# Attention kernel: the last two probability tiles of each half are added on VectorE, and TensorE's denominators take two sets of matmuls per half instead of three

## The chip, the core and the metric

The kernel runs on one core of a Trainium2 chip. A core has TensorE (PE in the profile, PEld for its weight loads), VectorE (DVE), ScalarE (ACT), GpSimd (POOL) and SyncE (SP), which here issues every transfer. All have their own instruction streams and meet at semaphores. The metric is the device time of one execution in microseconds (us).

## What is computed

The input x is 8 batches of 1024 tokens by 512 features. It is normalised by token; the result adds x, an attention block and a feed-forward block of ternary weights:

```python
xn = _layernorm(x, axis=-1)
x = x + _L0_attn_ref(xn, L0_attn_W_qkv, L0_attn_W_o) + _L0_ffn_ref(xn, L0_ffn_w_fc, L0_ffn_w_proj)
```

The attention has 16 heads of 32 features in each batch:

```python
scores = jnp.einsum('bhqd,bhkd->bhqk', Q, K) * D_H ** (-0.5)
attn = jax.nn.softmax(scores, axis=-1)
out = jnp.einsum('bhqk,bhkd->bhqd', attn, V)
```

The softmax divides each row of exponentials by its sum, the denominator. The change is in how these sums over the keys are formed.

## The kernel before, in words

Four stages follow one another: the weights (`weight_stage`), the tokens with the feed-forward block (`token_stage`), the attention (`attention_stage`), and the output projection (`output_stage`). Only the attention stage is touched.

**Groups, halves, units.** The 128 pairs of batch and head are taken four at a time: 32 groups (`GROUPS`), HG = 4 heads each. A group has two halves of 512 queries, and a half has 8 units, each with 128 keys (the keys lie on the partitions, the 512 queries along the free side). So a group has 16 units, w = 0 to 15; the first half is w = 0 to 7, the second w = 8 to 15. The probabilities of a unit are one tile `pr[:, w % 8]` of 128 x (4 heads x 512) float32, and there are 8 such slots.

**TensorE in one unit** (`body` under `@block.tensor`, L1019 to L1039). In this order: scores of head 0, one maxima matmul, scores of head 1, one maxima matmul, scores of head 2, then the denominators when the table `DEN` has an entry for this w, then the outputs of the unit before (`outputs`, L972), then a maxima matmul, scores of head 3, a maxima matmul. The maxima matmuls (`max_scores`, L985) are a second computation of scores, for a group ahead (the next one, and from w = 13 on the one after it), since the row maxima must be known before that group's exponentials. They are written to `psX`, which has three banks.

**VectorE** reduces each of these banks to row maxima (`maximum`, L919), 64 in a group, four in a unit. A maxima matmul waits on `max_done` until the reduction three before it is done (at the end of a group, two before: `bank_free`, L715). Between the reductions VectorE has a few small operations: `negate` at w = 13, `split_rows` at w = 14, `invert` at w = 7 and 15.

**ScalarE** takes the exponential of each scores bank (`exp`, L877) and copies outputs and denominators out of PSUM.

**GpSimd** adds the probability tiles 0 to 5 (`POOLED` = 6) of a half into `acc[:, hf]`, with five additions of 128 x 2048 (`add`, L849): the first at w % 8 = 1, once tiles 0 and 1 are there. It also multiplies the outputs by the inverse denominators (`normalise`, L858), at w = 2 and w = 9.

**The denominators** of a half are formed by TensorE in the following units (`denominators`, L1000): ones matrices times a probability tile, four matmuls of 32 output rows (one for each head) a set. `DEN_STEPS` is KT_N - POOLED + 1 = 3: one set for tile 6, one for tile 7, one for `acc`, all accumulated in `psM`. The table `DEN` puts them, for the second half of the group before, at w = 2, 3, 4, and for the first half of the same group at w = 10, 11, 12. ScalarE copies them out at w = 5 and 13.

The order of each engine is written out by hand in these `body` functions and tables. Two groups at the start and two at the end are unrolled, the 28 between them run in a loop of four groups a turn (`groups`, L739). In the last group there are no maxima any more, and behind it come the last denominators.

Of the kernel before, what the change touches and what calls it, by code (L numbers as in the profile page):

```python
# [28 lines left out]
ALU = mybir.AluOpType  # L29
# [25 lines left out]
HG = 4  # L55
GROUPS = B * H // HG
KT_N = L // P
UNITS = 2 * KT_N
# [3 lines left out]
POOLED = 6  # L62
# [10 lines left out]
def shift(g, d):  # L73
    return g + d if isinstance(g, int) else (g[0], g[1], g[2] + d)
# [576 lines left out]

DEN_STEPS = KT_N - POOLED + 1
X_LATE = 13
# [7 lines left out]
STORE = {3: (1, 0), 10: (1, 1)}  # L661
DEN = {2: (1, 1, 0), 3: (1, 1, 1), 4: (1, 1, 2), 10: (0, 0, 0), 11: (0, 0, 1), 12: (0, 0, 2)}
DEN_OUT = {5: (1, 1), 13: (0, 0)}
# [5 lines left out]
def attention_stage(nc, stack_dram, v_dram, ot_dram, den_dram, keep):  # L669
# [5 lines left out]
    with ExitStack() as ctx:  # L675
# [27 lines left out]
        s_full, exp_done, pv_done = sem("scores_full"), sem("exp_done"), sem("pv_done")  # L703
        added = sem("probs_added")
        den_stored, few_loaded, inverted = sem("den_stored"), sem("few_loaded"), sem("inverted")
# [212 lines left out]
        def _(dve):  # L918
# [13 lines left out]
            def split_rows(n):  # L932
# [5 lines left out]
                                               ALU.mult, ALU.subtract).then_inc(rows_ready, 1)  # L938

            def invert(g, hf):  # L940
                dve.wait_ge(few_loaded, lin(g, 32, 16 * hf + 16))
                wait(dve, inv_stored, lin(g, 32, 16 * hf - 16))
                nc.vector.reciprocal(rfew[:, hf, :], few[:, hf, :]).then_inc(inverted, 1)

            def body(g, units):
                for w in units:
                    for k, x in enumerate(maxima(g, w)):
                        if x:
                            maximum(*x)
                        if k == 0 and w == X_LATE and exists(shift(g, 1)):  # L950
                            negate(shift(g, 1))
                        if k == 0 and due(INVERT, g, w):
                            invert(*due(INVERT, g, w))
                        if k == 1 and w == ROWS_AT and exists(shift(g, 1)):
                            split_rows(shift(g, 1))

            nc.vector.memset(ones[:], AUG_UNIT).then_inc(ones_set, 1)
            groups(dve, body)
            invert(GROUPS - 1, 1)

        @block.tensor
        def _(pe):
# [37 lines left out]
            def denominators(g, hf, k):  # L1000

                if k == 0:
                    pe.wait_ge(exp_done, lin(g, PER_GROUP, HG * KT_N * (hf + 1)))
                    if hf == 0:
# [186 lines left out]
```

## Time and profile before

| | us |
|---|---|
| median of 3 runs | 3598.9 (3597.92 to 3601.58) |
| the profiled execution, whole | 3605.65 |
| its span, first to last instruction | 3603.8 |
| PE busy in the span | 3366.3 (93%) |
| DVE busy | 2345.0 (65%) |
| ACT busy | 1989.4 (55%) |
| POOL busy | 2076.2 (58%) |
| mean granted TensorE clock, share of full speed | 0.969 |

The attention stage takes from about 1619 us to 3362 us of the span. A busy engine is one that has an instruction in work; for PE, whose matmuls overlap, busy doesn't mean that it is at its peak. Instructions that follow one another closely on one engine overlap in the records by some hundredths of a microsecond; the distance from start to start is then what one takes of the engine's time.

### The profile page before, as it was taken

The numbers are of one execution on the slowest core, as the hardware profiler recorded it, in microseconds if no ns is written. First come the engines' busy times: TensorE is split into PE (matmuls) and PEld (weight loads), VectorE is DVE, ScalarE is ACT, GpSimd is POOL, SyncE is SP. The second block draws the span as 40 slices with busy tenths as digits, with TensorE's granted clock in tenths as the row PEclk, the third lists the DMA queues.
The fourth block names the chain that finished last, engine by engine and source line by source line (L and its number), as shares of the span: only waits on it lengthen the run. The fifth ranks groups of instructions, "written<-read, shape, count | busy, mean of one in ns | idle before, by whom it ended". The sixth has DMA issues, their size and how long they took to land. (4 is left out here: it accounts for less than half of the span.)

```text
span 3603.8 us, 57034 instructions
## 1 busy us (share of the span) xinstructions
PE 3366.3 (93%) x17648; PEld 1448.0 (40%) x17648; DVE 2345.0 (65%) x3431; ACT 1989.4 (55%) x2946; POOL 2076.2 (58%) x705
## 2 busy tenths in 40 slices
PE   3899999999999999989999999999999999999687
PEld 2444444444444444432333333333333333333466
DVE  6666666655666666668777777777777777773111
ACT  3444434433443443433877777777777777778111
POOL 0333332333332223314999898989989898999332
PEclk7999999999999999997999999999999999999799
DMA  4122222222222222133333333333233333321465
GB/s 163 71 76 86 71 86 72 85 85 78 79 81 89 81 80 72 82 79 68 81 70 68 78 73 69 72 78 71 68 78 75 65 75 74 76 64 31 147 226 198
DMA packets 376034, 308.49 MB, mean 86 GB/s; under 512 B 300672, under 2 KB 317056, under 8 KB 365440
## 3 DMA queue, kind: packets, MB, share of 16 engines
q1 hardware_dynamic: 375744, 304.69, 31.1%
q8 instruction: 174, 2.85, 0.3%
q14 instruction: 116, 0.95, 0.1%
HBM read 96.99 MB, written 139.46 MB: 66 GB/s over the span
## 5 line engine op out<-in xcount | busy, mean ns | idle before, releaser
L924 DVE TENSOR_REDUCE half_maxima<-scores_for_maxima 128x1 f32<-128x512 f32 x2048 | 1277.1, 682 | 370.1 <-PE scores_for_maxima L990 369.8
L887 ACT ACTIVATE probs<-scores,scalars 128x512 f32<-128x512 f32 x2048 | 1256.7, 689 | 423.8 <-PE scores L969 423.4
L855 POOL TENSOR_TENSOR probs_sum<-probs_sum,probs 128x2048 f32<-128x2048 f32 x256 | 1163.2, 4544 | 16.9
L990 PE MATMUL scores_for_maxima<-k_stackT,q_stackT 96*128 96x512 f16 x2048 | 804.1, 394 | 21.6 <-DMA q_stackT<-stack_scratch 11.2
L969 PE MATMUL scores<-q_stackT,k_stackT 98*128 98x512 f16 x2048 | 783.7, 385 | 27.6 <-issue 18.5
L981 PE MATMUL outputs<-probs,v_rows 128*32 128x512 f32 x4096 | 545.5, 605 | 1.2 <-ACT probs L887 0.8
L558 ACT ACTIVATE gelu_out<-psA,scalars 128x1024 f32<-128x1024 f32 x128 | 142.5, 1113 | 666.2 <-PE psA L607 666.2
L990 PEld LDWEIGHTS scores_for_maxima<-k_stackT,q_stackT 96*128 96x128 f16 x2048 | 200.5, 98 | 624.9 <-DVE half_maxima L924 468.1
L855 POOL TENSOR_TENSOR probs_sum<-probs 128x2048 f32<-128x2048 f32 x64 | 291.2, 4549 | 220.3 <-ACT probs L887 220.3
L969 PEld LDWEIGHTS scores<-q_stackT,k_stackT 98*128 98x128 f16 x2048 | 294.7, 145 | 241.5 <-ACT probs L887 46.5
L607 PE MATMUL psA<-x_hi,ternary_fcT 128*128 128x512 f16 x1024 | 388.2, 379 | 1.8 <-DVE x_lo L431 1.4
L607 PE MATMUL psA<-x_lo,ternary_fcT 128*128 128x512 f16 x1024 | 388.3, 379 | 0.0
L637 PE MATMUL psC<-ternary_projT,h_lo 128*128 128x512 f16 x1024 | 388.2, 379 | 0.0
L637 PE MATMUL psC<-ternary_projT,h_hi 128*128 128x512 f16 x1024 | 388.1, 379 | 0.0
L385 POOL TENSOR_TENSOR gelu_sum<-gelu_sum,gelu_out 128x1024 f32<-128x1024 f32 x96 | 256.4, 2671 | 194.9 <-ACT gelu_out L558 190.5
L385 POOL TENSOR_TENSOR gelu_sum<-gelu_out 128x1024 f32<-128x1024 f32 x16 | 41.0, 2563 | 554.2 <-ACT gelu_out L558 554.2
L593 PE MATMUL psB<-wqkvT_hi,x_hi 128*128 128x512 f16 x768 | 296.8, 386 | 50.7 <-DVE hi_hi_lo_hi_rows L424 50.6
L538 ACT ACTIVATE hi_hi_lo_hi_rows<-psB,qkv_scale 128x1024 f16<-128x1024 f32 x192 | 213.9, 1114 | 194.3 <-PE psB L593 194.3
L593 PE MATMUL psB<-wqkvT_lo,x_hi 128*128 128x512 f16 x768 | 296.8, 386 | 0.0
L593 PE MATMUL psB<-wqkvT_hi,x_lo 128*128 128x512 f16 x768 | 296.2, 386 | 0.0
L500 DVE SCALAR_TENSOR_TENSOR square_sum<-ternary_proj_sums,hidden_stats,psC 128x512 f32<-128x512 f32 x64 | 47.8, 747 | 319.2 <-PE psC L637 319.2
L454 DVE TENSOR_SCALAR h_hi<-gelu_out,scalars 128x1024 f16<-128x1024 f32 x128 | 167.7, 1310 | 134.1 <-ACT gelu_out L558 133.6
(123 smaller groups left out, 3313.2 us busy)
## 6 DMA issues: line engine op xcount, KB each, us to landing
stack_scratch<-hi_hi_lo_hi_rows SPq DMA_DIRECT2D x32, 1536.0 KB, 5.1
stack_scratch<-hi_hi_lo_hi_rows SPq DMA_DIRECT2D x32, 576.0 KB, 5.9
v_scratch<-v_rows_out SPq DMA_DIRECT2D x32, 576.0 KB, 6.9
x_rows<-in_L_attn_x SPq DMA_DIRECT2D x16, 1024.0 KB, 4.8
x_plus_ffn_scratch<-x_rows SPq DMA_DIRECT2D x16, 1024.0 KB, 3.9
v_rows<-v_scratch SPq DMA_DIRECT2D x32, 512.0 KB, 4.1
inverse_denominators<-denominators_scratch SPq DMA_DIRECT2D x256, 64.0 KB, 2.1
attention_scratch<-out_normed SPq DMA_DIRECT2D x64, 256.0 KB, 2.0
```

Source lines behind the costliest of these rows:

```text
L385: nc.gpsimd.tensor_tensor(gacc[:], g[:, 0, :] if j == 1 else gacc[:], g[:, j % 4, :], ALU.add).then_inc(g_added, 1)
L454: nc.vector.tensor_scalar(hh[:, pair, :], gj, S["inv1"], None, ALU.mult).then_inc(hh_ready, 1)
L538: nc.scalar.activation(stack[:, i % 2, heads, 0:2, :], rows.unsqueeze(2).to_broadcast([P, BANK // DH, 2, DH]), ACT.Copy, scale=rc[:, s, i: ...
L593: last = nc.tensor.matmul(psB[:, u % 2, :], xx[:, s, c, i * P:(i + 1) * P], keep[ww][:, c, cols], start=(k == 0), stop=(k == len(terms) - 1))
L607: last = nc.tensor.matmul(psA[:, 2 * (j % 2) + b, :], w, xx[:, s, c, :], start=(c == 0 and k == 0), stop=(c == CD - 1 and k == 1))
L637: last = nc.tensor.matmul(psC[:, (s + 5 + i) % 2, :], h[:, f, i * P:(i + 1) * P], keep["t2T"][:, f, :], start=(f == 0 and k == 0), stop=(f ...
L855: nc.gpsimd.tensor_tensor(acc[:, hf], pr[:, 0] if j == 1 else acc[:, hf], pr[:, j], ALU.add).then_inc(added, 1)
L887: nc.scalar.activation(pr[:, w % 8, h, :], psS[:, bank(HG * w + h), :], ACT.Exp, scale=keep["scal"]["escale"]).then_inc(exp_done, 1)
L924: nc.vector.tensor_reduce(mx[:, slot(n, 2), h, t, kh:kh + 1], psX[:, bank(r), :], axis=AX.X, op=ALU.max).then_inc(max_done, 1)
L969: nc.tensor.matmul(psS[:, bank(HG * w + h), :], kT[0:AUG, slot(g, 4), h, i:L:KT_N], qT[0:AUG, slot(g, 4), h, hf * BANK:(hf + 1) * BANK], s ...
L981: last = nc.tensor.matmul(psO[32 * h:32 * h + 32, :], v[:, slot(g, 2), h, i, :], pr[:, w % 8, h, :], start=(i == 0), stop=(i == KT_N - 1))
L990: nc.tensor.matmul(psX[:, bank(r), :], qT[0:STACK, slot(n, 4), h, t * P:(t + 1) * P], kT[0:STACK, slot(n, 4), h, kh * BANK:(kh + 1) * BANK ...
```

## The change

VectorE gets a new operation, `add_pair`: it adds tile 7 of a half onto tile 6, in place, 128 x 2048 float32 with both inputs in SBUF. A new table `PAIR` puts it after the second reduction of unit 9 (for the first half of the same group) and of unit 1 (for the second half of the group before), and once behind the last group. It waits until all exponentials of that half are done and until TensorE has used tile 6 for the outputs. TensorE's denominators have two sets, one for the summed tile and one for `acc`; the sets at w = 2 and w = 10 are gone, and the first of the two that are left waits for the new addition instead of for the exponentials.

```diff
-DEN_STEPS = KT_N - POOLED + 1
+DEN_STEPS = 2
...
-DEN = {2: (1, 1, 0), 3: (1, 1, 1), 4: (1, 1, 2), 10: (0, 0, 0), 11: (0, 0, 1), 12: (0, 0, 2)}
+PAIR = {1: (1, 1), 9: (0, 0)}
+DEN = {3: (1, 1, 0), 4: (1, 1, 1), 11: (0, 0, 0), 12: (0, 0, 1)}
...
-        added = sem("probs_added")
+        added, pair_added = sem("probs_added"), sem("last_pair_added")
...
+            def add_pair(g, hf):
+                dve.wait_ge(exp_done, lin(g, PER_GROUP, HG * KT_N * (hf + 1)))
+                dve.wait_ge(pv_done, lin(g, UNITS, 8 * hf + POOLED + 1))
+                nc.vector.tensor_tensor(pr[:, POOLED], pr[:, POOLED], pr[:, POOLED + 1], ALU.add).then_inc(pair_added, 1)
...
+                        if k == 1 and due(PAIR, g, w):
+                            add_pair(*due(PAIR, g, w))
...
             groups(dve, body)
+            add_pair(GROUPS - 1, 1)
             invert(GROUPS - 1, 1)
...
                 if k == 0:
-                    pe.wait_ge(exp_done, lin(g, PER_GROUP, HG * KT_N * (hf + 1)))
+                    pe.wait_ge(pair_added, lin(g, 2, hf + 1))
```

VectorE's order before, from unit 15 of the first group to unit 13 of the second (a row is an instruction, or so many equal ones):

```order
L924 TENSOR_REDUCE half_maxima<-scores_for_maxima 128x1 x3
L943 RECIPROCAL inverses_once<-denominators_once 128x16
L924 TENSOR_REDUCE half_maxima<-scores_for_maxima 128x1 x32
L943 RECIPROCAL inverses_once<-denominators_once 128x16
L924 TENSOR_REDUCE half_maxima<-scores_for_maxima 128x1 x24
L929 TENSOR_REDUCE negated_maxima<-half_maxima 128x32
```

and now the same stretch, where the lines of the kernel are one to six higher:

```order
L925 TENSOR_REDUCE half_maxima<-scores_for_maxima 128x1 x3
L949 RECIPROCAL inverses_once<-denominators_once 128x16
L925 TENSOR_REDUCE half_maxima<-scores_for_maxima 128x1 x9
L944 TENSOR_TENSOR probs<-probs 128x2048
L925 TENSOR_REDUCE half_maxima<-scores_for_maxima 128x1 x23
L949 RECIPROCAL inverses_once<-denominators_once 128x16
L925 TENSOR_REDUCE half_maxima<-scores_for_maxima 128x1 x9
L944 TENSOR_TENSOR probs<-probs 128x2048
L925 TENSOR_REDUCE half_maxima<-scores_for_maxima 128x1 x15
L930 TENSOR_REDUCE negated_maxima<-half_maxima 128x32
```

The new addition stands between reductions, once in each half, with 64 reductions for every two additions.

TensorE's order before, in unit 10 of a group, from its second maxima matmul (L1014 is a set of denominators, L981 the outputs of the unit before):

```order
L990 MATMUL scores_for_maxima<-k_stackT,q_stackT 128x512
L969 MATMUL scores<-q_stackT,k_stackT 128x512
L1014 MATMUL misc<-probs,ones 32x512 x4
L981 MATMUL outputs<-probs,v_rows 32x512 x4
L990 MATMUL scores_for_maxima<-k_stackT,q_stackT 128x512
```

and now, at the same place:

```order
L999 MATMUL scores_for_maxima<-k_stackT,q_stackT 128x512
L978 MATMUL scores<-q_stackT,k_stackT 128x512
L990 MATMUL outputs<-probs,v_rows 32x512 x4
L999 MATMUL scores_for_maxima<-k_stackT,q_stackT 128x512
L978 MATMUL scores<-q_stackT,k_stackT 128x512
```

One set of four matmuls has gone from unit 10, as from unit 2; nothing else of TensorE's order moved.

## Rows read from the trace of the kernel before

**Rows 1.** Page, costliest groups: busy us, mean ns | idle before, releaser.
```profile
L924 DVE TENSOR_REDUCE half_maxima<-scores_for_maxima 128x1 f32<-128x512 f32 x2048 | 1277.1, 682 | 370.1 <-PE scores_for_maxima L990 369.8
L855 POOL TENSOR_TENSOR probs_sum<-probs_sum,probs 128x2048 f32<-128x2048 f32 x256 | 1163.2, 4544 | 16.9
```
**Rows 2.** Windows: busy us of PE, PEld, DVE, ACT, POOL; clock, DMA. Group, last group.
```profile
2511.82:2563.47 51.65, 51.24 (x307) 18.28 (x306) 40.53 (x70) 40.67 (x69) 47.82 (x12) 1.00 0.36 74
3295.50:3347.70 52.20, 42.50 (x252) 12.05 (x250) 0.51 (x2) 39.01 (x66) 50.88 (x14) 0.99 0.08 22
```
**Rows 3.** Lines, shapes kept apart: denominator matmuls of tiles 6 and 7.
```profile
L1014 PE MATMUL misc<-probs,ones 128*32 128x512 f32 x1024 | 136.1, 604 | 0.0
```
**Rows 4.** Timeline (start us, us, instruction [idle before <-releaser]), PE and DVE, units 0 to 2.
```profile
2507.55 0.39 PE L990 MATMUL scores_for_maxima<-k_stackT,q_stackT 96*128 96x512 f16 x1
2507.98 2.48 DVE L924 TENSOR_REDUCE half_maxima<-scores_for_maxima 128x1 f32<-128x512 f32 x4 [0.70 <-PE scores_for_maxima L990]
2510.41 0.39 PE L990 MATMUL scores_for_maxima<-k_stackT,q_stackT 96*128 96x512 f16 x1
2510.84 2.49 DVE L924 TENSOR_REDUCE half_maxima<-scores_for_maxima 128x1 f32<-128x512 f32 x4 [0.38 <-PE scores_for_maxima L990]
2511.74 0.38 PE L990 MATMUL scores_for_maxima<-k_stackT,q_stackT 96*128 96x512 f16 x1
2512.26 1.07 PE L1014 MATMUL misc<-probs,ones 128*32 128x512 f32 x8
2514.12 0.39 PE L990 MATMUL scores_for_maxima<-k_stackT,q_stackT 96*128 96x512 f16 x1
```
**Rows 5.** Timeline of PE and DVE, units 12 and 13.
```profile
2495.67 1.89 DVE L924 TENSOR_REDUCE half_maxima<-scores_for_maxima 128x1 f32<-128x512 f32 x3 [1.22 <-PE scores_for_maxima L990]
2497.02 0.39 PE L990 MATMUL scores_for_maxima<-k_stackT,q_stackT 96*128 96x512 f16 x1 [0.29 <-DVE half_maxima L924]
2497.56 1.06 PE L981 MATMUL outputs<-probs,v_rows 128*32 128x512 f32 x8
```
**Rows 6.** Timeline of POOL, three halves.
```profile
2491.29 18.42 POOL L855 TENSOR_TENSOR probs_sum<-probs_sum,probs 128x2048 f32<-128x2048 f32 x4
2511.82 4.55 POOL L855 TENSOR_TENSOR probs_sum<-probs 128x2048 f32<-128x2048 f32 x1 [2.12 <-ACT probs L887]
...
2522.20 13.80 POOL L855 TENSOR_TENSOR probs_sum<-probs_sum,probs 128x2048 f32<-128x2048 f32 x3
2537.20 4.55 POOL L855 TENSOR_TENSOR probs_sum<-probs 128x2048 f32<-128x2048 f32 x1 [1.21 <-ACT probs L887]
```
**Rows 7.** Timeline of POOL and DVE in the token stage; a DVE addition without POOL.
```profile
795.18 5.11 POOL L385 TENSOR_TENSOR gelu_sum<-gelu_sum,gelu_out 128x1024 f32<-128x1024 f32 x2 [0.23 <-POOL qkv_scale L375]
798.01 3.37 DVE L440 TENSOR_TENSOR square_sum<-square_sum,gelu_squared 128x1024 f32<-128x1024 f32 x1
801.30 1.27 DVE L458 SCALAR_TENSOR_TENSOR h_lo<-gelu_out,scalars,h_hi 128x1024 f16<-128x1024 f32 x1
801.45 3.33 POOL L385 TENSOR_TENSOR gelu_sum<-gelu_sum,gelu_out 128x1024 f32<-128x1024 f32 x1 [1.16 <-ACT gelu_out L558]
...
3364.44 2.29 DVE L1136 TENSOR_TENSOR woT_lo<-woT,woT_hi 128x2048 fp32r<-128x2048 f32 x1 [10.49 <-ACT woT_hi L1099]
```
**Rows 8.** Timeline of PE where the loop starts its next turn.
```profile
2611.92 0.44 PE L969 MATMUL scores<-q_stackT,k_stackT 98*128 98x512 f16 x1 [3.42 <-issue]
...
2613.79 1.94 PE L981 MATMUL outputs<-probs,v_rows 128*32 128x512 f32 x8
```
**Rows 9.** Windows, columns as in rows 2: just behind that gap.
```profile
2613.00:2615.00 2.00, 2.00 (x11) 0.20 (x8) 1.00 (x2) 1.50 (x3) 0.00 (x0) 0.50 0.80 131
```
**Rows 10.** Timeline of POOL and PE in the last group.
```profile
3299.05 4.56 POOL L855 TENSOR_TENSOR probs_sum<-probs 128x2048 f32<-128x2048 f32 x1 [0.46 <-ACT probs L887]
3323.37 4.56 POOL L855 TENSOR_TENSOR probs_sum<-probs 128x2048 f32<-128x2048 f32 x1
3347.75 1.93 PE L1014 MATMUL misc<-probs_sum,ones 128*32 128x512 f32 x8 [4.05 <-POOL probs_sum L855]
```

## The prediction

> **What bounds the kernel now.** I began with the page's groups, for the load of the engine that gets the new work, then took the windows of one group, and then the timeline of the units in which something changes. In the steady part a group takes 51.65 us; TensorE is busy for 51.24 us of it, VectorE for 40.53, ScalarE for 40.67, GpSimd for 47.82, and the granted clock is 1.00 [rows 2]. TensorE is the bound, GpSimd is close behind. VectorE looks free: it waits 369.8 us in all for maxima banks [rows 1]. The question is in what pieces that idle time lies. The timeline shows it: four reductions in 2.48 us, then 0.38 us of idle in a unit of 2.86 us, which is the distance of the maxima matmuls at 2507.55 and 2510.41 [rows 4]. TensorE, in turn, has three banks for VectorE to be late in.
>
> What happens when they don't suffice is to be seen once in each group already. Near its end two maxima matmuls share a bank at a distance of two. There TensorE idles 0.29 us until a reduction is done, and starts at 2497.02, 0.06 us after the second of three reductions ended (the three end at 2497.56, and they lie 0.60 apart) [rows 5]. The outputs come 0.54 us behind that matmul; in the undisturbed unit the next set comes 0.52 us behind it [rows 4, 5]. So TensorE makes up for none of the delay: scores and outputs stand behind the waiting matmul in its order, and whoever delays that matmul delays the group.
>
> **What goes.** A set of denominators in unit 2 stretches the distance of the maxima matmuls from 2.86 to 3.71 us (2510.41 to 2514.12), so it takes 0.85 us of TensorE [rows 4]. The 1024 records of tile sets are 64 halves by 16 [rows 3]; half of them go. Of the 64 removed sets 61 lie in groups 0 to 30, where TensorE is the bound (unit 10 of 31 groups, unit 2 of 30): 61 x 0.85 = 51.9 us saved. The other three lie in the last group or behind it, where GpSimd's additions are waited for, and save nothing.
>
> **What comes.** The trace has one VectorE addition of just this shape, two float32 inputs of 128 x 2048 in SBUF, with GpSimd idle: 2.29 us [rows 7]. As instructions overlap in the records by 0.08 us (a reduction is recorded at 682 ns, four of them at 2.48 us), it takes 2.2 us of the engine.
>
> In unit 1 it starts when the fourth reduction ends, at 2510.46. The next reduction, of the bank filled by the matmul at 2510.41, now starts at 2510.84; it would start at 2512.67 to 2512.75 and end 0.60 later. The matmul three further on, now at 2511.74, needs that bank: it would start at 2513.33 to 2513.41, later by 1.6 to 1.7 us; I take 1.65. The slack of the three banks is thus about 0.6 us, and the rest of the addition comes through. It happens in unit 2, in front of the place from which the 0.85 us go, so nothing of it is covered by that gap. Behind it VectorE has caught up within a unit: its four reductions need 2.48 us of TensorE's 2.86. For the size the bounds are 0 (the banks hide all) and 2.29 (they hide nothing); the worked value is near the second because the 0.6 is read from the same rows. 61 additions by 1.65: 100.7 us. Net of the saved sets, 48.8 us.
>
> **The addition and GpSimd.** In the token stage a VectorE addition starts at 798.01 while GpSimd is in the second of two additions that end at 800.29. It lasts 3.37 us and ends at 801.38, 1.09 us after GpSimd. The other way round, GpSimd's addition at 801.45 starts beside a VectorE operation at 801.30 of 1.27 us and takes 3.33 us, where the pair before took 5.11 for two [rows 7]. So the two take turns. The Trainium skill has a rule for this ("SBUF — State Buffer", section "Who interferes with whom"): a VectorE instruction with two SBUF inputs and a GpSimd instruction that reads SBUF exclude each other, and the later one blocks until the first is done. By that rule, the trace agrees; without it, the next two terms would be nothing.
>
> Where does the new addition meet GpSimd? In unit 1 it asks at 2510.46, and GpSimd is idle since 2509.71. It goes first, and GpSimd's first addition, now at 2511.82, begins about 2512.7 [rows 4, 6]. From there GpSimd needs 24.18 us (2511.82 to 2536.00). The next addition on VectorE asks 25.38 us after this one before the change, and 25.38 - 0.85 + 1.65 = 26.18 after. GpSimd ends 2.29 + 24.18 = 26.47 after it, so VectorE stands for about 0.28 us, which goes to TensorE whole: 31 x 0.28 = 8.7 us. From unit 9 to unit 1 the distance is 26.27 + 0.80 + 0.28 = 27.35, and GpSimd is done before. This balances itself: a longer wait lengthens the half and frees GpSimd earlier. GpSimd's own lateness costs nothing there; its sum is used at unit 4 or 12, three units after its last addition.
>
> In the last group there are no maxima, and GpSimd is the bound: 50.88 us busy of 52.20 [rows 2], 0.46 us idle ahead of its first addition, none ahead of the second half's, and the last set of denominators waits 4.05 us for it [rows 10]. Each of three VectorE additions takes 2.2 us of its time: 6.6 less the 0.46, 6.1 us. Bounds 0 and 3 x 2.29.
>
> New waits: the first denominator set waits for the addition, two units after it, and behind it on TensorE stand that unit's outputs; it is done 5 us before, so nothing. The addition's own two waits (exponentials and outputs of the half before) are over by unit 1. ScalarE and the queue of SP are passed by nothing.
>
> **The sum.** -51.9 + 100.7 + 8.7 + 6.1 = 63.6 us. The profiled execution took 3605.65 us, so 3669.3; it lies 6.75 us above the median of the runs, so 3662.5 beside 3598.9. I forecast 3662 us, slower by 1.8%. Its own range: with 1.5 us of delay, no wait for GpSimd and no tail, 61 x 0.65 = 40 us, 3639; with 1.8 us, 0.6 us of wait in both halves and 7 us of tail, 58 + 37 + 7 = 102, 3701.
>
> **Rivals.**
>
> The banks hide the addition. VectorE has 51.65 - 40.53 = 11.1 us of idle in a group and gets 4.6; if TensorE could run on, through banks or by having the reductions ahead, only the saving stays: 3598.9 - 51.9 + 6.1 = 3553 us. For it speaks the idle total; against it that this idle comes in pieces of 0.4 to 1.2 us behind TensorE's outputs, and that a delay of the banks showed in TensorE at once [rows 5]. It decides this way if less than 0.85 us of each addition reaches TensorE. Chance 0.06.
>
> The addition waits behind whole GpSimd additions. If VectorE's request falls in the middle of one in each half, it stands on average half of 4.54 us [rows 1], 2.27 x 61 = 138 us in place of the 8.7: 3792 us. For it: GpSimd is busy for 93% of a group. Against: its idle lies just where the addition asks [rows 6]. Chance 0.07. The rule named above is the same for both; they differ in when the request falls.
>
> The clock. Where TensorE stood 3.42 us at the loop's edge, the clock behind it was granted at 0.50 (1.2 GHz in place of 2.4), and a set of outputs took 1.94 us in place of 1.06 [rows 8, 9]. If the new stands of 1.65 us do the same, each costs some 0.9 us for outputs and 0.4 for scores: 61 x 1.3 = 79, 3742 us. Against: every stand in the trace that brought this was twice as long. Chance 0.03.
>
> It cancels: if the delay is 0.85 to 0.95 us (a shorter addition, or slack that I don't see), the time stays within 10 us. Chance 0.04.
>
> **Chances and range.** Forecast 0.80, the rivals 0.06, 0.07, 0.03 and 0.04. Within 0.2% (7 us, about what a measurement of this kernel tells from no change) I put 0.03; faster 0.07, with the rest of the cancelling case; slower 0.90. The range 3635 to 3708 holds the forecast's own and leaves out the far cases.
>
> **What the changed profile would show.** 64 VectorE additions of 128 x 2048, in the steady part of 2.3 us, those in unit 9 a little longer. A wait of TensorE for the reductions of 1.4 to 1.7 us in units 2 and 10, ahead of the second maxima matmul. A group of 51.65 + 2 x 0.80 + 0.28 = 53.5 us. GpSimd's first addition of a half recorded near 5.4 us. Units 2 and 10 without a denominator set. GpSimd's chain in the last group longer by about 6 us. I am wrong if a group is shorter than 51.65 us, if VectorE's additions have a mean over 3.5 us, or if the granted clock in the steady part falls below 0.95.

## The result, and the profile after

The changed kernel takes 3681.14 us in the median of 4 runs (3676.39 to 3688.44); the kernel before, run beside it, 3599.77 us (3597.92 to 3601.58, 4 runs). The ratio is 1.0225, with a 95% interval of 1.021 to 1.024: the change costs 81.4 us. The prediction was 3662 us in a range of 3635 to 3708. The profiled execution of the changed kernel is its fastest one, with a span of 3674.5 us, so the two traces are only 70.7 us apart (3603.8 before), and that is the difference the rows below have to explain.

Of the page's groups after the change, columns as in [rows 1]:

```profile
L925 DVE TENSOR_REDUCE half_maxima<-scores_for_maxima 128x1 f32<-128x512 f32 x2048 | 1277.0, 680 | 300.8 <-PE scores_for_maxima L999 299.9
L999 PE MATMUL scores_for_maxima<-k_stackT,q_stackT 96*128 96x512 f16 x2048 | 808.9, 396 | 110.4 <-DVE half_maxima L925 98.9
L856 POOL TENSOR_TENSOR probs_sum<-probs 128x2048 f32<-128x2048 f32 x64 | 333.6, 5213 | 239.7 <-ACT probs L888 239.7
```

VectorE's idle time ahead of its reductions has fallen by 70 us, and TensorE now waits 98.9 us for VectorE ahead of the maxima matmuls. GpSimd's first addition of a half is recorded at 5213 ns on average: the part above the 4.55 us of [rows 6] is its wait for VectorE.

One undisturbed group in a window, columns as in [rows 2], and the matmuls that answer to [rows 3]:

```profile
2135.41:2188.59 53.18, 49.88 (x290) 17.70 (x289) 44.77 (x72) 40.94 (x69) 49.25 (x13) 1.00 0.34 71
```
```profile
L1023 PE MATMUL misc<-probs,ones 128*32 128x512 f32 x512 | 68.3, 605 | 3.4 <-DVE probs L944 3.4
```

The group takes 53.18 us in place of 51.65. TensorE is busy for 1.36 us less and is idle for 3.3 us instead of 0.4: it is no longer the full engine, though the group has become longer. The clock is 1.00 in both.

The place where it happens, at the change from unit 9 to unit 10, in the timeline of VectorE and TensorE; it answers to [rows 4]:

```profile
2513.73 2.48 DVE L925 TENSOR_REDUCE half_maxima<-scores_for_maxima 128x1 f32<-128x512 f32 x4 [0.36 <-PE scores_for_maxima L999]
2516.13 2.33 DVE L944 TENSOR_TENSOR probs<-probs 128x2048 f32<-128x2048 f32 x1
2518.39 2.47 DVE L925 TENSOR_REDUCE half_maxima<-scores_for_maxima 128x1 f32<-128x512 f32 x4
```
```profile
2517.05 0.38 PE L999 MATMUL scores_for_maxima<-k_stackT,q_stackT 96*128 96x512 f16 x1
2519.12 0.39 PE L999 MATMUL scores_for_maxima<-k_stackT,q_stackT 96*128 96x512 f16 x1 [1.47 <-DVE half_maxima L925]
2519.66 1.06 PE L990 MATMUL outputs<-probs,v_rows 128*32 128x512 f32 x8
```

Behind the outputs of unit 9 the maxima matmuls come every 0.44 us (2516.16, 2516.61, 2517.05); the fourth of them, the second of unit 10, was due at 2517.49 and starts at 2519.12, 1.63 us late. The recorded wait is 1.47 us. The outputs stand 0.54 us behind it and are late by the same. The addition begins when VectorE's fourth reduction ends, and the reduction behind it is the one whose bank TensorE wants.

The same event, summed over the attention stage (view of waits, TensorE, in total, times, longest):

```profile
PE scores_for_maxima L999 <- DVE half_maxima L925: 94.3, 90, 1.6
PE scores L978 <- issue: 17.9, 6, 3.3
PE scores L978 <- DMA q_stackT<-maxima_rows: 5.0, 7, 1.3
```

The third line was not there before. Transfers of the maxima rows, which had been in time, are late in some groups. This does not come with the addition: the same view of g_sets_alone (below; two sets, nothing on VectorE) has it too, and in b_add_alone (three sets and the addition) there is none.

```profile
PE scores L975 <- DMA q_stackT<-maxima_rows: 5.0, 6, 1.1
```

### The profile page after: what moved, and what is told of

The parts are those of the page before. It is cut to its first block and busy times, and to the rows that moved or that the text cites. A ratio compares the mean times of both kernels' runs of the same rounds, so it can differ in the third digit from the quotient of the medians.

```text
span 3674.5 us, 56159 instructions
## 1 busy us (share of the span) xinstructions
PE 3341.1 (91%) x17136; PEld 1434.4 (39%) x17136; DVE 2485.4 (68%) x3495; ACT 1998.8 (54%) x2946; POOL 2112.1 (57%) x705
## 5 line engine op out<-in xcount | busy, mean ns | idle before, releaser
L999 PE MATMUL scores_for_maxima<-k_stackT,q_stackT 96*128 96x512 f16 x2048 | 808.9, 396 | 110.4 <-DVE half_maxima L925 98.9
L990 PE MATMUL outputs<-probs,v_rows 128*32 128x512 f32 x4096 | 553.1, 612 | 1.2 <-ACT probs L888 0.8
L856 POOL TENSOR_TENSOR probs_sum<-probs 128x2048 f32<-128x2048 f32 x64 | 333.6, 5213 | 239.7 <-ACT probs L888 239.7
L593 PE MATMUL psB<-wqkvT_hi,x_hi 128*128 128x512 f16 x768 | 297.0, 387 | 46.8 <-DVE hi_hi_lo_hi_rows L424 46.8
```

Of the source, the lines that this page charges most:

```text
L593: last = nc.tensor.matmul(psB[:, u % 2, :], xx[:, s, c, i * P:(i + 1) * P], keep[ww][:, c, cols], start=(k == 0), stop=(k == len(terms) - 1))
L856: nc.gpsimd.tensor_tensor(acc[:, hf], pr[:, 0] if j == 1 else acc[:, hf], pr[:, j], ALU.add).then_inc(added, 1)
L990: last = nc.tensor.matmul(psO[32 * h:32 * h + 32, :], v[:, slot(g, 2), h, i, :], pr[:, w % 8, h, :], start=(i == 0), stop=(i == KT_N - 1))
L999: nc.tensor.matmul(psX[:, bank(r), :], qT[0:STACK, slot(n, 4), h, t * P:(t + 1) * P], kT[0:STACK, slot(n, 4), h, kh * BANK:(kh + 1) * BANK ...
```

## The experiments

All times of "the kernel before" are from the same chip and job. GpSimd's first addition of a half marks a half; its distance to the next is called the spacing. There are two, because unit 1 to unit 9 and unit 9 to the next unit 1 differ: 25.37 and 26.28 us before, 26.10 and 27.07 after. These are the usual values, those of the halves in which nothing else is late: between the second half of group 0 and that of group 30, 28 and 21 of 30 have them before, 25 and 12 of 30 after.

**The sets alone.** Two sets per half, nothing on VectorE. First try, which leaves tile 7 out of the denominators and puts a multiplication where the reciprocal of the denominators was:

```
-DEN = {2: (1, 1, 0), 3: (1, 1, 1), 4: (1, 1, 2), 10: (0, 0, 0), 11: (0, 0, 1), 12: (0, 0, 2)}
+DEN = {3: (1, 1, 0), 4: (1, 1, 1), 11: (0, 0, 0), 12: (0, 0, 1)}
...
-                nc.vector.reciprocal(rfew[:, hf, :], few[:, hf, :]).then_inc(inverted, 1)
+                nc.vector.tensor_scalar(rfew[:, hf, :], few[:, hf, :], 1.0, None, ALU.mult).then_inc(inverted, 1)
```

> Two denominator sets, no addition on VectorE (tile 7 is left out of the sums, and the inverses are replaced by the sums themselves). Bank theory (the addition costs its time on VectorE less 0.6 us of slack, and that is the whole loss): TensorE is the bound without it, so 61 sets of 0.85 us go: 3600 - 52 = 3548 us, a group of 49.95 us. GpSimd theory (the loss comes from GpSimd, which is pushed to its limit of 24.2 us a half): the halves shrink to no less than about 25.4 us, since GpSimd cannot do better with its idle of 1.2 and 2.1 us: 3570 us or more.

Measured: 3681.73 us (3677.05 to 3686.94), ratio 1.0232 (1.0215 to 1.0249). That looked like a refutation: as slow as the whole change without its addition. The trace says otherwise. The tile view of the multiplication (min/median/max ns) in this kernel:

```profile
L949 DVE TENSOR_SCALAR inverses_once<-denominators_once x64: 175/2311/3184, 1709.0 to 3425.3; 128x16 f32<-128x16 f32 x64
```

and of the reciprocal in the changed kernel:

```profile
L949 DVE RECIPROCAL inverses_once<-denominators_once x64: 240/242/254, 1718.9 to 3422.0; 128x16 f32<-128x16 f32 x64
```

An operation on 16 columns that needs 175 ns stood for 2311 ns in the median, as long as the addition that it was to be compared without. It stood in the middle of GpSimd's additions and waited for them: in each of 16 looked at, every fourth, it started inside a GpSimd addition and ended 0.03 to 0.04 us after it. The reciprocal of the same shape at the same place never waits. The two other kernels with this multiplication, c_add_half and f_reduce_same, have the same fault and say nothing about their question:

> The changed kernel with an addition of half the size, heads 0 and 1 only (the sums of heads 2 and 3 lack tile 7, and the inverses are replaced by the sums themselves). Bank theory: it holds VectorE for 1.13 us, 0.6 of it is slack, so TensorE is delayed by 0.5 us and saves 0.85: 61 x -0.35 = -21, 3 us in the last group: 3582 us, faster than before. Without any slack (the whole addition reaches TensorE): 61 x 0.28 + 3 = +20: 3620 us. If the loss is a fixed price for an additional operation there, whatever its size: 3660 us or more.

Measured: 3662.55 us (3659.49 to 3668.62), ratio 1.0179 (1.0162 to 1.0196).

> The changed kernel with a maximum over tile 6 (128 x 2048, one input) at the place of the addition, about as long on VectorE, but with one SBUF input (tile 7 is left out of the sums, and the inverses are replaced by the sums themselves). Bank theory: the steady part is as in the changed kernel, groups of 53.2 us, since the addition hardly waited for GpSimd there; the last group loses its 6 us: 3681 - 6 = 3675 us. If the loss comes from VectorE and GpSimd excluding each other, it goes with the second input: 3560 to 3600 us.

Measured: 3684.46 us (3674.03 to 3693.0), ratio 1.0231 (1.0205 to 1.0257).

So all three were made anew, with the reciprocal kept, and 1e-20 added by ScalarE where it copies the denominators:

```
-                nc.scalar.copy(den[:], psM[:]).then_inc(d_out, 1)
+                nc.scalar.activation(den[:], psM[:], ACT.Copy, bias=1e-20).then_inc(d_out, 1)
```

> As a_sets_alone, but with the reciprocals on VectorE left as they are (243 ns, never waiting for GpSimd) and 1e-20 added to the denominators by ScalarE's copy, so that none is zero; tile 7 is left out of the sums. In a_sets_alone the operation in their place had a median of 2311 ns, since it waited for GpSimd, and cost as much as the addition. Bank theory: with it gone, 61 sets of 0.85 us are saved: 3600 - 52 = 3548 us, groups of 49.95 us, with up to 15 us more if the clock drops without the sets' work. GpSimd theory: 3570 us or more, halves no shorter than 25.4 us.

Measured: 3555.07 us (3554.74 to 3556.63) against 3602.96, ratio 0.987 (0.9854 to 0.9887). Timeline of GpSimd:

```profile
2483.82 4.55 POOL L856 TENSOR_TENSOR probs_sum<-probs 128x2048 f32<-128x2048 f32 x1 [2.19 <-ACT probs L888]
2508.33 4.54 POOL L856 TENSOR_TENSOR probs_sum<-probs 128x2048 f32<-128x2048 f32 x1 [0.34 <-ACT probs L888]
2533.76 4.55 POOL L856 TENSOR_TENSOR probs_sum<-probs 128x2048 f32<-128x2048 f32 x1 [1.27 <-ACT probs L888]
```

Spacings 24.51 and 25.43 us, 0.86 and 0.85 shorter than before. The half of the change that saves does save, by the value read from [rows 4]. In all it saved 47.9 us and not 51.9; the 5.0 us of waits for maxima rows shown above are about the difference.

**The addition alone.** The addition goes to a tile of its own, the three sets stay, and the second of them waits for it as in the changed kernel:

```
+                nc.vector.tensor_tensor(spare[:], pr[:, POOLED], pr[:, POOLED + 1], ALU.add).then_inc(pair_added, 1)
...
+                if k == 1:
+                    pe.wait_ge(pair_added, lin(g, 2, hf + 1))
```

> The addition, into a tile of its own, and all three denominator sets as before. Bank theory: each of 61 additions delays TensorE by 1.65 us, 6 us in the last group, and some 10 us for low clock and late maxima rows as in the changed kernel: 3600 + 101 + 6 + 10 = 3717 us. If part of the loss needs the missing sets (less of TensorE's own work to cover VectorE's), the addition alone costs less: under 3690 us.

Measured: 3718.03 us (3717.77 to 3721.08), ratio 1.0328 (1.031 to 1.0345). Timeline of GpSimd:

```profile
2485.46 5.24 POOL L857 TENSOR_TENSOR probs_sum<-probs 128x2048 f32<-128x2048 f32 x1 [2.04 <-ACT probs L889]
2513.35 5.23 POOL L857 TENSOR_TENSOR probs_sum<-probs 128x2048 f32<-128x2048 f32 x1 [3.04 <-ACT probs L889]
2540.31 5.24 POOL L857 TENSOR_TENSOR probs_sum<-probs 128x2048 f32<-128x2048 f32 x1 [2.06 <-ACT probs L889]
```

27.89 and 26.96 us: 1.60 more than before in either half. A set stands right behind TensorE's wait here, and covers nothing of it.

**Half of the addition.** Two of the four heads of tile 7, 128 x 1024; the others are left out of the denominators:

```
+                nc.vector.tensor_tensor(pr[:, POOLED, 0:2], pr[:, POOLED, 0:2], pr[:, POOLED + 1, 0:2], ALU.add).then_inc(pair_added, 1)
```

> As c_add_half with the reciprocals left as they are and 1e-20 added to the denominators by ScalarE; heads 2 and 3 lack tile 7 in their sums. Bank theory: the addition of 128 x 1024 (1.21 us, 1.13 of VectorE's time) less 0.6 us of slack delays TensorE by 0.5 us where it saves 0.85: 3600 - 21 + 3 = 3582 us. Without slack: 3620 us. A fixed price for an operation there: 3660 us or more.

Measured: 3606.94 us (3601.66 to 3616.2, 10 runs), ratio 1.0015 (1.0004 to 1.0026). The spacing from unit 1 to 9 is 25.04, 0.53 more than without the addition, as a shorter one should give (1.22 us of addition, less 0.08 of overlap in the records and 0.6 of slack, is 0.54). From unit 9 to 1 it is 26.39, 0.96 more. Tile view:

```profile
L944 DVE TENSOR_TENSOR probs<-probs x64: 1214/1574/3623, 1692.7 to 3336.2; 128x1024 f32<-128x1024 f32 x64
```

The additions in unit 1 take 1.22 us, those in unit 9 (2482.49) 1.64: the halves are now short enough that GpSimd, 24.2 us after its first addition, is not done when VectorE asks. That is the balancing wait of the prediction. It comes where the delay is small, and was all but gone at the real delay. The expectation was 25 us too low: 7 of them were lacking in the sets alone already (3555 against 3548), and this wait, 0.42 us in 31 halves, is 13; the rest lies behind the second half of group 0 (29.05 us) and in the last group.

**The length without the exclusion.** A max-reduction over tile 6 takes as long as the addition but has one input in SBUF; tile 7 is left out of the denominators:

```
+                nc.vector.tensor_reduce(spare[:], pr[:, POOLED].rearrange("p h q -> p (h q)"), axis=AX.X, op=ALU.max).then_inc(pair_added, 1)
```

> As f_reduce_same with the reciprocals left as they are and 1e-20 added to the denominators by ScalarE: a maximum over tile 6 in the place of the addition, 2275 ns with one SBUF input, that never waited for GpSimd; tile 7 is left out of the sums. Bank theory: the steady halves are those of the changed kernel, 26.1 and 27.07 us, and the last group loses its 6 us: 3675 us. If the loss comes from VectorE and GpSimd excluding each other: 3550 to 3600 us.

Measured: 3657.16 us (3655.05 to 3657.97), ratio 1.0151 (1.0134 to 1.0168). Tile view:

```profile
L945 DVE TENSOR_REDUCE pair_max<-probs x64: 2274/2276/2287, 1692.8 to 3388.6; 128x1 f32<-128x2048 f32 x64
```

None of the 64 waits for GpSimd, and none of GpSimd's first additions is lengthened (4.53 us). Yet the spacings are 26.09 and 27.02, against 26.10 and 27.07 with the addition. So in the usual halves the exclusion costs 0.01 to 0.05 us. The stand is VectorE's time, not GpSimd's. The exclusion costs elsewhere: the spacing behind the second half of group 0, the first with an addition in it that meets GpSimd at work, is 26.71 us here and 31.28 in the changed kernel, and the last spacing in the last group is 24.34 us here, 24.32 before and 26.19 after. The expectation of 3675 us was 18 too high, since it took off only the last group. Of the 19.2 us between the two traces, 4.6 lie in that one half of group 0, 5.6 behind the start of group 30's second half and 1.8 in the usual spacings; the rest lies mostly in halves with a low clock, of which there are more in the changed kernel's trace.

**The place.** The addition behind the fourth maxima reduction of its unit instead of the second, all else as in the changed kernel:

```
-                        if k == 1 and due(PAIR, g, w):
+                        if k == 3 and due(PAIR, g, w):
```

> The changed kernel with the addition two reductions later, behind the fourth of unit 1 or 9. There GpSimd's first addition of the half has started 0.26 us before. Bank theory with exclusion: VectorE stands 4.2 us more, the next reduction ends about 5.4 us later than TensorE needs it: 61 x (5.4 - 0.85) = 278, 6 in the last group: about 3884 us, additions recorded near 6.5 us. Banks alone, without exclusion: the stand is 1.25 us in place of 1.65: about 3655 us, additions of 2.3 us.

Measured: 4049.38 us (2 runs), ratio 1.1241 (1.1213 to 1.127). Tile view, the timeline of TensorE, and a window behind its stand:

```profile
L944 DVE TENSOR_TENSOR probs<-probs x64: 3141/6447/6515, 1697.0 to 3783.5; 128x2048 f32<-128x2048 f32 x64
```
```profile
2441.17 0.61 PE L999 MATMUL scores_for_maxima<-k_stackT,q_stackT 96*128 96x512 f16 x1 [5.28 <-DVE half_maxima L925]
```
```profile
2442.00:2443.00 1.00, 1.00 (x4) 0.47 (x3) 1.00 (x3) 0.61 (x1) 1.00 (x1) 0.50 0.30 115
```

Two reductions later, GpSimd's first addition has begun, and VectorE's takes 6.45 us instead of 2.3. TensorE stands for 5.28 us, and the clock behind it is granted at 0.50. The expectation of 3884 us held the wait but not the clock: the whole execution has a mean granted clock of 0.912, the changed kernel's 0.963. The missing share times the span is 357 us against 136, an estimate of what the clock took in each; the 221 us between them are more than the 165 that the expectation lacks.

The max-reduction at that later place shows that the place alone does not cost this:

> Part left out: tile 7 of each half is not added to the denominators, and 1e-20 is added to them instead; a max-reduction over tile 6 (128x2048, one input, 2275 ns, never waits for GpSimd) stands in its place, but two reductions later, behind the 4th reduction of unit 1/9, where the addition of d_add_later stood. Place theory (a place costs what the next reduction's bank lacks, and d lost its time because its addition there waited for GpSimd, 6.45 us instead of 2.3): the reduction stalls TensorE by about 1.25 us a half instead of the 1.60 of i_reduce_same, 61 x 0.35 = 21 us less than i's 3657: about 3636 us. Rival (the place itself is bad, whatever the length): the stand is 3 to 5 us as in d, and the time 3900 us or more.

Measured: 3671.65 us (3667.8 to 3675.5, 2 runs), ratio 1.0192 (1.0169 to 1.0216). Both expectations missed. The rival is out, but the 0.35 us did not come either: spacings 26.11 and 27.03, those of i_reduce_same. TensorE in the timeline:

```profile
2524.81 0.39 PE L1000 MATMUL scores_for_maxima<-k_stackT,q_stackT 96*128 96x512 f16 x1
...
2526.52 0.39 PE L1000 MATMUL scores_for_maxima<-k_stackT,q_stackT 96*128 96x512 f16 x1 [1.11 <-DVE half_maxima L926]
...
2527.12 0.39 PE L1000 MATMUL scores_for_maxima<-k_stackT,q_stackT 96*128 96x512 f16 x1
...
2527.72 0.39 PE L1000 MATMUL scores_for_maxima<-k_stackT,q_stackT 96*128 96x512 f16 x1
```

The recorded wait is shorter, 1.11 us. The matmul that waits comes 1.71 us after the one before it instead of 0.44, so it is 1.27 us late, and the next two come after 0.60 us each, VectorE's pace, so 0.16 later each time: 1.27 + 2 x 0.16 = 1.59. The delay is the same, and only a part of it is recorded as a wait. The slack is the same at both places that were tried. The median is nevertheless 14.5 us above that of i_reduce_same; the profiled executions have mean granted clocks of 0.961 and 0.965, which at this length are some 15 us.

More slack is to be had in a unit where TensorE has a set to do. The same max-reduction in unit 3 and 11:

```
-PAIR = {1: (1, 1), 9: (0, 0)}
+PAIR = {3: (1, 1), 11: (0, 0)}
```

(Here the accumulator's set, one unit later, is the one that waits for the reduction; the set beside it waits for the exponentials.)

> Part left out: as in e_reduce_later, tile 7 is not added to the denominators. The same max-reduction stands at unit 3/11, behind the second reduction, in a unit where TensorE has a set of denominators (0.85 us, read from g_sets_alone) to do beside it. Place theory: that set and the bank's 0.6 us of slack cover part of 2.28 us, a stand of about 0.75 us a half is left: 61 x 0.75 = 46 on g's 3555: about 3601 us, level with the kernel before. Rival (place does not matter, the reduction's length is paid wherever it stands): 3657 us as i_reduce_same.

Measured: 3603.85 us (3595.4 to 3607.97, 10 runs) against 3601.8, ratio 1.0001 (0.9992 to 1.0011). Timeline of TensorE:

```profile
2492.79 0.39 PE L1000 MATMUL scores_for_maxima<-k_stackT,q_stackT 96*128 96x512 f16 x1 [0.57 <-DVE half_maxima L926]
...
2518.96 0.39 PE L1000 MATMUL scores_for_maxima<-k_stackT,q_stackT 96*128 96x512 f16 x1 [0.57 <-DVE half_maxima L926]
2544.22 0.39 PE L1000 MATMUL scores_for_maxima<-k_stackT,q_stackT 96*128 96x512 f16 x1 [0.57 <-DVE half_maxima L926]
```

26.17 and 25.26 us, 0.75 above those without VectorE's work, as worked out. A set beside it covers its 0.85 us. With this cover and without the exclusion, 2.28 us of VectorE's time come out level with the set that they replace. GpSimd is busy at this place, so the real addition would have to wait for it as in d_add_later; that was not run.

**The real addition, with its sets moved.** Both kernels compute everything. In m_set_behind the accumulator's set stands in unit 2 and 10, right behind the stand, and the pair's in unit 3 and 11; in n_set_ahead they are one unit earlier still (units 1 and 2, 9 and 10), the first one beside the addition. The edit of m_set_behind:

```
-DEN = {3: (1, 1, 0), 4: (1, 1, 1), 11: (0, 0, 0), 12: (0, 0, 1)}
+DEN = {2: (1, 1, 0), 3: (1, 1, 1), 10: (0, 0, 0), 11: (0, 0, 1)}
-                part = pr[:, POOLED + k] if k < DEN_STEPS - 1 else acc[:, hf]
+                part = acc[:, hf] if k == 0 else pr[:, POOLED]
```

> The changed kernel with its two sets of denominators one unit earlier, the accumulator's in unit 2/10 (right behind TensorE's stand) and the pair's in unit 3/11. If it is the lack of a set right behind the stand that lets the clock drop there, the drops outside the loop's edges go and the time is about 3668 us with a spread of a few us; the spacing of the halves stays at 26.1 and 27.1 us. Rival (the drops come from the stand alone, or the set's place does nothing): 3681 us with the spread of the changed kernel.

Measured: 3688.86 us (3680.47 to 3693.1) against 3601.8, ratio 1.0244 (1.0227 to 1.0261): the rival. Spacings 26.11 and 27.16. Timeline and window of TensorE behind one stand:

```profile
1747.28 0.39 PE L999 MATMUL scores_for_maxima<-k_stackT,q_stackT 96*128 96x512 f16 x1 [1.57 <-DVE half_maxima L925]
...
1747.82 1.61 PE L1023 MATMUL misc<-probs_sum,ones 128*32 128x512 f32 x8
1749.18 1.95 PE L990 MATMUL outputs<-probs,v_rows 128*32 128x512 f32 x8
```
```profile
1749.00:1750.00 1.00, 1.00 (x8) 0.22 (x4) 0.02 (x1) 0.00 (x0) 1.00 (x1) 0.50 0.00 0
```

A part of the set and the outputs behind it run at the lower clock. A set there does not keep the clock up.

> The changed kernel with the accumulator's set ahead of the stand, in unit 1/9 beside VectorE's addition, and the pair's in unit 2/10. Place theory: the set gives TensorE 0.85 us of work beside the addition, but it waits for GpSimd's 5th addition (0.2 us in unit 1, about 1.1 us in unit 9), and GpSimd's 24.2 us and the addition's 2.0 us in one half are a floor of 26.2 us against 26.59 now: at most 0.39 x 61 = 24 us less than the changed kernel, about 3655 us, still slower than the kernel before (25.83 a half). Rival (the set ahead only moves the wait): 3681 us or more.

Measured: 3737.99 us (3730.35 to 3750.73), ratio 1.0376 (1.0345 to 1.0408): the rival's direction, and worse than it said. Timeline of GpSimd and TensorE:

```profile
2484.80 4.52 POOL L856 TENSOR_TENSOR probs_sum<-probs_sum,probs 128x2048 f32<-128x2048 f32 x1
...
2489.38 1.06 PE L1023 MATMUL misc<-probs_sum,ones 128*32 128x512 f32 x8 [2.29 <-POOL probs_sum L856]
...
2492.64 4.55 POOL L856 TENSOR_TENSOR probs_sum<-probs 128x2048 f32<-128x2048 f32 x1 [3.32 <-ACT probs L888]
...
2520.09 4.56 POOL L856 TENSOR_TENSOR probs_sum<-probs 128x2048 f32<-128x2048 f32 x1 [3.32 <-ACT probs L888]
```

A circle has closed. TensorE's set waits 2.29 us for GpSimd's fifth addition; scores and exponentials stand behind the set, and GpSimd's next first addition comes 3.32 us after its last one ended. 24.13 us of GpSimd and 3.32 of idle are 27.45, the spacing of 31 of the 60 halves; most others are longer, and the mean granted clock is 0.953, the lowest of the versions but d_add_later. The floor in the expectation, 24.2 and 2.0, left this return path out.

## Why the prediction was right, and where it wasn't

The 81.4 us that were measured lie 18 us above the 63.6 of the sum, inside the range. The mechanism held: VectorE's time less the banks' slack reaches TensorE whole, against a smaller saving. The closeness is in part luck. In the trace the terms of the sum come to 51.4 us (45.6 in the steady part, 5.8 in the last group), 12 less than forecast, and 30 us came from what the sum had not. With its terms at their measured size the forecast would have been 3650 us.

**The saved sets**, -51.9 us: right. 0.85 us each, by g_sets_alone.

**The stand**, +100.7 us: right. 1.60 us in place of 1.65 (b_add_alone: 61 x 1.60 = 97.6). That it is VectorE's length less the banks' slack, without any part of GpSimd in it, i_reduce_same shows, and h_add_half gives the same slack with half the length; that a set behind the stand makes up for none of it, b_add_alone shows; that a set beside VectorE's work covers its own length, j_reduce_beside_set shows.

**The wait for GpSimd in unit 9**, +8.7 us: too large. The additions there take 2.31 to 2.33 us against 2.28 in unit 1, so 0.05 and not 0.28, some 1.5 us in all. The step that failed is the 2.29 + 24.18 = 26.47 us: it set the whole length of an undelayed GpSimd addition behind the end of VectorE's. One that has waited is recorded with 5.28 us from 2517.57 and ends at 2522.85, 4.39 us after VectorE's at 2518.46, not 4.55. That is 0.16 of the missing 0.23; the rest is within what records overlap:

```profile
2517.57 5.28 POOL L856 TENSOR_TENSOR probs_sum<-probs 128x2048 f32<-128x2048 f32 x1 [1.26 <-ACT probs L888]
```

**The last group**, +6.1 us: right. From GpSimd's start of group 30's second half to its last operation the changed kernel takes 3415.87 - 3336.65 = 79.22 us; before it was 73.4, so 5.8 more. GpSimd's chain there, answering to [rows 10]; the blocks with a blocked addition in them are some 2 us longer than the 18.4 of four and the 13.8 of three in [rows 6]:

```profile
3343.18 20.47 POOL L856 TENSOR_TENSOR probs_sum<-probs_sum,probs 128x2048 f32<-128x2048 f32 x4
...
3374.03 15.81 POOL L856 TENSOR_TENSOR probs_sum<-probs_sum,probs 128x2048 f32<-128x2048 f32 x3
```

**New waits**, nothing: nearly. The sets' wait for the addition never ends last in the steady part (3.4 us in all, in the last group). The 5.0 us for the transfers of the maxima rows were not seen. They come with the removal of the sets (g_sets_alone has them, b_add_alone has not), but two sets are not enough for them: j_reduce_beside_set has none. Why was not looked into.

**What the forecast lacked.** In the two profiled executions, the halves that take longer than the usual ones of their kernel add 46.8 us after the change (18 halves) and 27.2 us before (7 halves). These 19.6 us lie in three places, and most of them are the rival "the clock".

The first is the spacing behind the second half of group 0 (1695.83 to 1727.11), 4.2 us longer than usual: there GpSimd has run through from the half before, and the two additions wait for one another:

```profile
1693.93 4.10 DVE L944 TENSOR_TENSOR probs<-probs 128x2048 f32<-128x2048 f32 x1
```
```profile
1695.83 6.57 POOL L856 TENSOR_TENSOR probs_sum<-probs 128x2048 f32<-128x2048 f32 x1
```

TensorE waits 3.15 us at 1698.68 in place of some 1.6, and the clock behind that wait is low, 0.89 over the whole stretch:

```profile
1697.00:1727.00 30.00, 27.86 (x145) 9.03 (x145) 23.17 (x38) 19.68 (x33) 23.57 (x5) 0.89 0.13 29
```

The second is the six edges of the loop. They cost 31.9 in place of 27.0 us, 4.9 more, and that is clock too. Two of these halves before, and one after (clock: third number from the end):

```profile
2379.56:2408.51 28.95, 25.87 (x155) 9.19 (x154) 20.64 (x37) 20.54 (x35) 23.88 (x6) 1.00 0.20 45
2800.34:2830.90 30.56, 27.49 (x155) 9.35 (x154) 20.74 (x37) 20.59 (x35) 23.88 (x7) 0.94 0.19 42
```
```profile
2624.22:2657.59 33.37, 28.33 (x146) 9.14 (x145) 22.97 (x38) 20.78 (x35) 24.57 (x7) 0.90 0.22 40
```

The share that is missing from a full clock, times the length, is an estimate of what the clock takes: nothing, 1.8 and 3.3 us. Over the six edges it adds to 10 us before and 16 after. In the last of the three windows the clock is low twice, behind the edge and behind the new stand of 1.46 us, where a set of outputs takes 1.94 us in place of 1.06:

```profile
2625.75 0.39 PE L999 MATMUL scores_for_maxima<-k_stackT,q_stackT 96*128 96x512 f16 x1 [1.46 <-DVE half_maxima L925]
...
2626.39 1.94 PE L990 MATMUL outputs<-probs,v_rows 128*32 128x512 f32 x8
```

The third is eleven other halves that take 0.2 to 2.7 us more than usual, 10.7 in all, where before there was one with 0.16. Four of them have the clock low behind a stand of some 1.5 us. TensorE behind the stand at 1754.82, where it had waited 1.59 us, and the windows:

```profile
1755.35 1.63 PE L990 MATMUL outputs<-probs,v_rows 128*32 128x512 f32 x8
1756.91 0.61 PE L999 MATMUL scores_for_maxima<-k_stackT,q_stackT 96*128 96x512 f16 x1
```
```profile
1755.00:1756.00 1.00, 1.00 (x10) 0.16 (x8) 1.00 (x3) 0.54 (x1) 1.00 (x1) 0.86 0.00 0
1756.00:1757.00 1.00, 1.00 (x9) 0.09 (x2) 0.55 (x1) 0.15 (x1) 1.00 (x1) 0.50 0.00 0
1757.00:1758.00 1.00, 1.00 (x3) 0.39 (x4) 0.44 (x1) 0.01 (x1) 1.00 (x1) 0.50 0.00 0
1758.00:1759.00 1.00, 1.00 (x3) 0.32 (x2) 0.84 (x2) 0.83 (x2) 1.00 (x2) 0.50 0.00 0
```

The shares missing from a full clock add to 0.14 + 3 x 0.50 = 1.64 us, and the half, 28.75 us, is 1.68 longer than usual. Seven of the eleven hold one late transfer of maxima rows each (the 5.0 us above), and one of these has both. By these estimates some 16 us of the 19.6 are clock, and 4 are late rows.

The prediction put this rival at 1.3 us a stand if every stand did it, and gave it 0.03 since all stands with a drop had been twice as long. That reading was loose: the trace before has a drop behind 2.78 us of issue (2822.77, second window above) and none behind 2.79 (2402.01, first window), so the length alone did not decide there either. After the change, six of the 60 stands of 1.4 to 1.6 us behind group 0 have one, at 1.6 to 1.7 us each, and e_reduce_later has drops behind 1.11 us (0.94 in its half of 28.68 us from 1806.51). Most stands of this length have none, as the one at 2519.12.

**The sum.** From the second half of group 0 to the second of group 30 are 60 spacings. At their usual values they give 30 x 0.79 + 30 x 0.73 = 45.6 us, the longer ones 19.6, and some halves behind the loop's edges are shorter than usual (25.75 to 25.96 in place of 26.10), -1.4 by difference: the starts are 1640.82 us apart (1695.83 to 3336.65) in place of 1576.99, 63.8 more. The last group adds 5.8, what comes behind it 2.5, and the stage begins 1.4 us earlier: 70.7 us, the difference of the spans. The last 10.7 us up to the medians' 81.4 are in executions without a trace: the changed kernel's median is 4.8 us above its profiled execution, and the kernel before's 5.9 below its own. For each execution of the changed kernel its mean granted clock is known: 0.963 in the profiled one, 0.960 to 0.961 in the other three. The 0.2 to 0.3% between them are 7 to 11 us, and these three took 4.5 to 12.1 us longer, so the clock is the likely cause there too, as far as three digits can tell. It isn't settled why one stand lets the clock fall and the next does not: b_add_alone, with the same stands and a set behind each, stays within 3.3 us, while m_set_behind, also with a set behind each, spreads over 12.6.

**No version here beats the kernel before.** One addition costs TensorE 1.60 us and frees 0.85. Only g_sets_alone is faster, and it leaves tile 7 out. With the addition beside GpSimd's own work, GpSimd's 24.2 us and the addition's 2.0 make 26.2 a half, which is more than the 25.83 of before; whether fewer GpSimd additions would open a way was not tried.

**The exclusion.** The runs bear out that VectorE's addition and GpSimd's take turns: 6.45 us in d_add_later against 2.28. They add two cases. A float32 multiplication by a constant from SBUF to SBUF, with one input, waits as well (2311 ns for 16 columns); a max-reduction of 128 x 2048 does not (2274 to 2287). The Trainium skill ("SBUF — State Buffer", section "Who interferes with whom") names both: `tensor_scalar` can enter a mode that takes the ports shared with GpSimd, while `tensor_reduce` on trn2 never contends. The traces agree with both sentences.

## What to carry to other kernels

Work given to an engine that is idle in short pieces is not hidden by the sum of those pieces. Here it was paid at its length, less the slack of the buffers between it and the engine that bounds the kernel, at both places of the unit that were tried; so count what a unit's slack is before counting the group's, and look for a unit where the bounding engine has something of its own to do.

A recorded wait can be smaller than the delay: compare the distances of a repeating instruction (here GpSimd's first addition of a half) and not the sums of waits. A stand-in operation in an experiment has properties of its own; look first at how long it took. And where many short waits are added to an engine whose clock can fall, compare the granted clock of the two traces before explaining what is left over: here it was most of it.

## What the runs showed of the hardware

- VectorE's multiplication of 128 x 16 float32 by a constant, SBUF to SBUF, waited for GpSimd's additions: 175 ns at least, 2311 in the median, 3184 at most. The reciprocal of the same shape at the same place took 240 to 254 ns.
- A GpSimd addition that has waited for VectorE ends 4.39 us behind it, where one alone takes 4.55: some 0.16 us of it lies beside the wait.
- The granted clock of TensorE fell to 0.50 behind six of the 60 stands of 1.4 to 1.6 us that follow group 0 in the changed kernel, and 1.6 to 1.7 us were lost each time; behind the others it stayed at 1.00. At the loop's edges of the kernel before it fell behind a gap of 2.78 us and not behind one of 2.79. Behind the stand of 5.28 us quoted from d_add_later it was 0.50 at once.
